# Column sums of attention probabilities: from GpSimd additions to TensorE products in four quadrants of one bank

## The chip, the cores and the metric

The kernel runs on one core of a Trainium2 chip. The metric is the device time of one execution in microseconds (us), from inputs in HBM to the output in HBM. Engines are named as in the profile: PE is TensorE, DVE is VectorE, ACT is ScalarE, POOL is GpSimd, SP is SyncE, which here only issues transfers.

## What is computed

The input `x` has 8 batches of 512 tokens with 128 channels. Four blocks follow each other, each with a residual: a causal attention with 16 heads of 8 channels and a distance bias, a gated feed-forward layer, a second attention over a compressed set of keys, and the feed-forward layer again. The second attention has to choose 51 of the 512 tokens first, and for that it computes the full attention's probabilities, from which only three statistics are kept:

```python
scores = jax.nn.softmax(jnp.einsum('bhqd,bhkd->bhqk', q, k) * scale, axis=-1)
# inside _heavy_hitter_indices(scores, S):
entropy = -jnp.sum(scores * jnp.log(jnp.clip(scores, 1e-08)), axis=-1)
max_attn = scores.max(axis=-1)
influence = scores.sum(axis=-2)
importance = -entropy.mean(axis=1) * 0.4 + max_attn.mean(axis=1) * 0.3 + influence.mean(axis=1) * 0.3
_, idx = jax.lax.top_k(importance, k)          # k = 51
```

`influence` is the column sum: for each key, the sum of its probabilities over all 512 queries and 16 heads. It is the part that the change computes in another way.

## The kernel before

The program is a software pipeline over the batches, written out by hand. One pass of `one_pass(i, a, p, m, s)` works on up to four batches at once: `p` projects batch i+1, `a` is the causal attention of batch i with its feed-forward layer, `m` is the full attention and the selection for batch i-1, and `s` is the small attention of batch i-2 with its feed-forward layer. Eight passes have the part `m`: the first has no `s`, the next five are the loop body and have all four parts, the seventh has no `p`, the eighth has neither `a` nor `p`. Every pass ends in a barrier of all engines.

Every engine has its own instruction stream in program order, and the streams meet only in semaphores. All of them count the same steps `n` from 0 to 74. Steps 0 to 63 each handle one tile of the full attention: 128 queries of one head against 512 keys (`h, t = n // 4, n % 4`). In a loop pass the other parts are put at fixed steps between them: the last eight heads of the causal row maxima in steps 0 to 7 (DVE line 866, after PE lines 1145 and 1148), the small attention's heads in steps 8 to 20 (PE lines 1397 and 1197), the causal attention in steps 20 to 49 (five tiles in three steps: PE line 1165 with its mask 1167, ACT line 776, PE line 1183), and from step 50 the projection, the layer norms and the feed-forward layers. In step 60 POOL computes the last bf16 parts of the next batch's queries and keys (line 560). SP then writes them to DRAM and reads them back into the causal stacks, 12 transfers of 128 KB each, and the pass doesn't end before these have landed.

One tile of the full attention goes this way:

- PE computes the scores one step ahead, in step n-1 (line 1229), into one of four PSUM banks, the ring 0, 1, 2, 6. It first waits until the tile four before has left the bank: `pe.wait_ge(s_bn, n - RN + 1)`, where `s_bn` counts entropies. The operands lie in partitions 64 and up; those of the causal scores lie in the lower 64.
- DVE takes the row maxima (line 947) at the head of its step n.
- ACT computes the exponentials into one of eight slots of `E` (named `setup` in the profile, line 747) with their row sums `Z`, and then the logarithm of the sums (line 750). POOL makes a threshold from it (line 606).
- DVE computes the entropy's sum from the bank, the threshold and `E` (line 902) in step n+2, directly behind the maxima of that step. After the fourth tile of a head it inverts the sums into `rz` (line 906).
- In step n+6 the slot of `E` is multiplied by `rz`, by ACT for tiles 0 to 13 and 46 to 55 (line 693) and by DVE for the others (line 919), and POOL adds the slot to the sum `psum` (line 580, 60 times in a pass). The four tiles of the last head are scaled and added by DVE (lines 958 and 962).
- When step 63 is over, PE multiplies `psum` and the last head's sum by a column of ones (lines 1311 and 1313). DVE makes the importance, the ranks and the selection from it, and PE gathers the chosen tokens (lines 1327 and 1330).

## Time and profile before

| | |
|---|---|
| median of 3 runs | 2352.26 us |
| all runs | 2352.26, 2664.49, 2349.68 us |
| profiled execution, first to last instruction | 2347.5 us |
| PE busy (matmuls) | 1731.0 us, 74% |
| DVE busy | 1492.3 us, 64% |
| ACT busy | 1121.6 us, 48% |
| POOL busy | 892.7 us, 38% |
| granted PE clock, mean | 0.757 of full speed |

The page gives no other time of the profiled execution than its span; the median of the runs is 4.8 us above that span. A busy share is an average over all stages of all passes. No engine is near 100%, so the table alone doesn't say what bounds the kernel. The granted clock stands at one of two levels, 1.2 GHz (0.50) and 2.4 GHz (1.00); a mean between them tells how a stretch is divided.

### The profile page before, as it was taken

The page shows a single profiled execution, that of the slowest core. Times are in us where ns is not written, and L with a number is a line of the kernel's source. Part 1 is how long each engine was busy: PE and PEld are TensorE (multiplying, and loading weights), DVE is VectorE, ACT ScalarE, POOL GpSimd, SP SyncE. Part 2 cuts the span into 40 slices and gives each one's busy share as a digit, 9 for nine tenths or more (in the row PEclk, how much of TensorE's full clock was granted, in tenths as well). Part 3 has the DMA queues.
Part 4 walks back from the last instruction along what each step waited for, and adds up shares of the span by engine and source line. Part 5 has one row for each costly group of instructions (what it writes and reads, how often), then busy time and mean ns, then how long its engine had stood idle before and what let it go on. Part 6 is the DMA issues. An engine that isn't in the chain of part 4 may idle for free. (4 is left out here: it accounts for less than half of the span.)

```text
span 2347.5 us, 25009 instructions
## 1 busy us (share of the span) xinstructions
PE 1731.0 (74%) x6733; PEld 734.6 (31%) x6733; DVE 1492.3 (64%) x3701; ACT 1121.6 (48%) x2726; POOL 892.7 (38%) x1252
## 2 busy tenths in 40 slices
PE   1686479668986799568976799668977799647537
PEld 1222233333333332333334332433334332322122
DVE  0401388847886677757875677757876677647931
ACT  1033167516772277416672376516672377446603
POOL 2001146513553155514562154514562155425700
PEclk9998559756987599756987589756987589656557
DMA  3002300250004200240005100240005100130010
GB/s 61 13 2 37 53 2 1 38 75 4 1 5 87 29 3 1 50 69 4 1 12 84 24 3 1 46 72 4 1 5 90 20 3 1 24 51 1 5 24 5
DMA packets 64106, 59.35 MB, mean 25 GB/s; under 512 B 10400, under 2 KB 61648, under 8 KB 63952
## 3 DMA queue, kind: packets, MB, share of 16 engines
q1 hardware_dynamic: 63952, 57.57, 15.1%
q8 instruction: 63, 1.03, 0.2%
q14 instruction: 91, 0.75, 0.1%
HBM read 39.10 MB, written 18.27 MB: 24 GB/s over the span
## 5 line engine op out<-in xcount | busy, mean ns | idle before, releaser
L580 POOL TENSOR_TENSOR psum<-psum,setup 128x512 f32<-128x512 f32 x480 | 614.1, 1279 | 55.5 <-ACT setup L693 52.1
L947 DVE TENSOR_REDUCE nmB<-bank 128x1 f32<-128x512 f32 x512 | 348.2, 680 | 290.7 <-PE bank L1229 289.8
L747 ACT ACTIVATE setup<-bank,nmB 128x512 f32<-128x512 f32 x512 | 349.8, 683 | 283.4 <-DVE nmB L947 252.7
L606 POOL TENSOR_TENSOR thr<-lnZ,nmB 128x1 f32<-128x1 f32 x512 | 102.1, 199 | 790.3 <-ACT lnZ L750 786.9
L902 DVE SCALAR_TENSOR_TENSOR junk<-bank,thr,setup 128x512 f32<-128x512 f32 x512 | 378.6, 739 | 20.5 <-POOL thr L606 18.8
L1229 PE MATMUL bank<-k_stacks,q_stacks 48*128 48x512 bf16 x512 | 236.8, 470 | 181.1 <-DMA k_stacks<-part_dram 111.0
L1183 PE MATMUL bank<-pT,vA 128*9 128x512 f32 (+3 forms) x1024 | 342.4, 440 | 10.8 <-ACT ov L686 10.6
L866 DVE TENSOR_REDUCE nm<-bank 128x1 f32<-128x512 f32 (+3 forms) x512 | 225.6, 482 | 127.6 <-PE bank L1148 124.7
L1145 PE MATMUL bank<-k_stacks,q_stacks 52*128 52x512 bf16 (+3 forms) x512 | 217.4, 425 | 120.0 <-PEq L1476 59.2
L776 ACT ACTIVATE pT<-bank 128x512 f32<-128x512 f32 (+1 forms) x384 | 198.8, 521 | 190.9 <-PE bank L1167 188.8
L919 DVE TENSOR_SCALAR setup<-setup,rz 128x512 f32<-128x512 f32 x288 | 195.0, 677 | 0.0
L1229 PEld LDWEIGHTS bank<-k_stacks,q_stacks 48*128 48x128 bf16 x512 | 47.7, 96 | 418.5 <-DVE junk L902 167.7
L1165 PE MATMUL bank<-q_stacks,k_stacks 55*128 55x512 bf16 (+3 forms) x512 | 159.8, 312 | 21.4 <-ACT pT L776 11.9
L1148 PE MATMUL bank<-maskqk,identb 128*128 128x128 bf16 x512 | 143.3, 280 | 0.0
L693 ACT ACTIVATE setup<-setup,rz 128x512 f32<-128x512 f32 x192 | 135.6, 706 | 0.0
L1197 PE MATMUL bank<-p,vsm 115*9 115x512 f32 x256 | 124.6, 722 | 4.4 <-ACT ov L686 3.6
L1167 PE MATMUL bank<-maskkq,identb 128*128 128x128 bf16 x512 | 118.6, 232 | 0.0
L750 ACT ACTIVATE lnZ<-Z 128x1 f32<-128x1 f32 x512 | 103.9, 203 | 16.2
L875 DVE RECIPROCAL rzo<-bank 128x16 f32<-128x16 f32 x64 | 16.3, 254 | 146.6 <-PE bank L1216 146.6
L1145 PEld LDWEIGHTS bank<-k_stacks,q_stacks 52*128 52x128 bf16 x512 | 51.9, 101 | 182.4 <-issue 90.9
L763 ACT ACTIVATE p<-bank 115x512 f32<-115x512 f32 x128 | 72.2, 584 | 66.5 <-PE bank L1397 33.8
L747 ACT ACTIVATION_READ_ACCUMULATOR setup<-bank,nmB 128x1 f32 x512 | 101.7, 199 | 0.0
(184 smaller groups left out, 2370.5 us busy)
## 6 DMA issues: line engine op xcount, KB each, us to landing
part_dram<-part SPq DMA_DIRECT2D x16, 768.0 KB, 3.3
q_stacks<-part_dram SPq DMA_DIRECT2D x96, 128.0 KB
k_stacks<-part_dram SPq DMA_DIRECT2D x96, 128.0 KB
qsm<-part_dram SPq DMA_DIRECT2D x48, 128.0 KB
x<-in_L_attn_a_x_dram SPq DMA_DIRECT2D x8, 256.0 KB, 3.9
x_dram<-x SPq DMA_DIRECT2D x8, 256.0 KB, 10.2
x2s<-x_dram SPq DMA_DIRECT2D x8, 256.0 KB, 11.4
out_dram<-x SPq DMA_DIRECT2D x8, 256.0 KB, 2.3
```

What stands on the lines that cost most here:

```text
L580: pool.tensor_tensor(psum[:, :], psum[:, :], E[:, n % NE, :], ALU.add).then_inc(s_bi, 1)
L747: act.activation(E[:, n % NE, :], RING[n % RN][:, :], ACT.Exp, bias=nmB[:, h, t:t + 1], accum_out=Z[:, h, t:t + 1]).then_inc(s_be, 1)
L776: act.activation(pT[h % 2][:, c * T:c * T + WIDTH[c]], bank[3 + u % 2][:, 0:WIDTH[c]], ACT.Exp).then_inc(s_p[0], 1)
L866: last = dve.tensor_reduce(nm[0][:, t, h:h + 1], bank[a1_bank(u)][:, at:at + (t + 1) * P], AX_X, ALU.max, negate=True)
L902: dve.scalar_tensor_tensor(out=junk[:, :], in0=RING[n % RN][:, :], scalar=thr[:, h, t:t + 1], in1=E[:, n % NE, :], op0=ALU.max, op1=ALU.mu ...
L919: dve.tensor_scalar(E[:, n % NE, :], E[:, n % NE, :], rz[:, h, t:t + 1], None, ALU.mult).then_inc(s_scv, 1)
L947: dve.tensor_reduce(nmB[:, h, t:t + 1], RING[n % RN][:, :], AX_X, ALU.max, negate=True).then_inc(s_bm, 1)
L1145: pe.matmul(bank[a1_bank(u)][:, at:at + (t + 1) * P], qst[0][0:A_SC, h, t * P:(t + 1) * P], kst[0][0:A_SC, h, 0:(t + 1) * P], start=True, ...
L1148: last = pe.matmul(bank[a1_bank(u)][:, at + t * P:at + (t + 1) * P], identb[:, :], maskqk[:, :], start=False, stop=True, skip_group_check= ...
L1165: pe.matmul(bank[3 + u % 2][:, at:at + w], kst[0][0:A_MX, h, k * P:(k + 1) * P], qst[0][0:A_MX, h, k * P:T], start=True, stop=True)
L1183: last = pe.matmul(bank[5][q:q + HD + 1, k * P:T], vA[:, k, h, :], pT[h % 2][:, c * T + at:c * T + at + T - k * P], start=(k == 0), stop=T ...
L1229: pe.matmul(RING[n % RN][:, :], qst[1][0:B_SC, h, t * P:(t + 1) * P], kst[1][0:B_SC, h, :], start=True, stop=True).then_inc(s_bs, 1)
```

## The change

Nobody multiplies the slots of `E` by `rz` any more, and nobody adds them up. Instead PE forms the column sums: for each head, four products with `rz` of one tile as the stationary operand (128 rows, one column) and the raw exponentials of that tile as the moving operand (512 columns, f32). Tile t of a head writes partition 32t of bank 6, which stays one accumulation over all 16 heads. So the four products of a head lie in four different column quadrants of the array. Bank 6 leaves the ring of scores, which has three banks now. At the end ACT copies the bank, and PE adds the four rows by a product with `quads`, a column that is one in partitions 0, 32, 64 and 96 and zero elsewhere. Beside that three things move: the entropy of tile n is computed in step n+1 in place of n+2, it stands at the end of DVE's step and no longer behind the maxima, and the inverted sums of a head come in the next step's head. POOL keeps the thresholds and its other work.

```diff
-        RING = (bank[0], bank[1], bank[2], bank[6])
+        RING = (bank[0], bank[1], bank[2])
+        INFL = bank[6]
...
-        INFL_LAG = 6
+        INFL_LAG = 5
...
-        ON_ACT = [n for n in range(LAST) if n < 14 or 46 <= n < 56]
-        ON_DVE = [n for n in range(LAST) if n not in ON_ACT]
...
+        ENT_FIRST = False
...
-                    def influence(n):
...
-                        pool.tensor_tensor(psum[:, :], psum[:, :], E[:, n % NE, :], ALU.add).then_inc(s_bi, 1)
...
-                    def probabilities(n):
...
-                        act.activation(E[:, n % NE, :], E[:, n % NE, :], ACT.Copy, scale=rz[:, h, t:t + 1]
-                                       ).then_inc(s_sc, 1)
...
-                                act.wait_ge(s_bi, n - NE + 2)
+                                act.wait_ge(s_bi, (n - NE) // NT + 1)
...
+                        if m and n == M_TAIL:
+
+                            act.wait_ge(s_bi, H)
+                            act.activation(infl[:, :], INFL[:, :], ACT.Copy).then_inc(s_icp, 1)
...
-                        if m and 2 <= n < NMAIN + 2:
-                            entropy(n - 2)
-                        if m and n - INFL_LAG in ON_DVE:
-                            probabilities(n - INFL_LAG)
+                        if m and 0 < n <= NMAIN and n % NT == 0:
+
+                            dve.wait_ge(s_be, n)
+                            dve.reciprocal(rz[:, n // NT - 1, :], Z[:, n // NT - 1, :]).then_inc(s_brz, 1)
...
-                                dve.tensor_scalar(E[:, LAST % NE, :], E[:, LAST % NE, :], rz[:, H - 1, 0:1], None,
-                                                  ALU.mult).then_inc(s_last, 1)
-                                for t in range(1, NT):
...
+                        if m and not ENT_FIRST and 0 < n <= NMAIN:
+                            entropy(n - 1)
...
+                    def influence(h):
+
+                        if h == 0:
+                            pe.wait_ge(s_vt[1], 2)
+                        pe.wait_ge(s_brz, h + 1)
+                        for t in range(NT):
+                            last = pe.matmul(INFL[32 * t:32 * t + 1, :], rz[:, h, t:t + 1], E[:, (NT * h + t) % NE, :],
+                                             start=(h == 0), stop=(h == H - 1))
+                        last.then_inc(s_bi, 1)
...
+                        if m and n >= INFL_LAG and (n - INFL_LAG) % NT == 0 and (n - INFL_LAG) // NT < H:
+                            influence((n - INFL_LAG) // NT)
...
+                                pe.wait_ge(s_icp, 1)
+                                pe.wait_ge(s_bn, NMAIN)
                                 for t in range(NT):
-                                    pe.matmul(bank[0][:, t:t + 1], psum[:, t * P:(t + 1) * P], onesf[:, 0:1],
-                                              start=True, stop=False)
-                                    last = pe.matmul(bank[0][:, t:t + 1], E[:, LAST % NE, t * P:(t + 1) * P],
-                                                     onesf[:, 0:1], start=False, stop=True)
+                                    last = pe.matmul(bank[0][:, t:t + 1], infl[:, t * P:(t + 1) * P], quads[:, :],
+                                                     start=True, stop=True)
```

The order of the instructions on two engines of a loop pass shows the moves. First DVE in steps 1 and 2, before; `nmB` are a tile's maxima, `nm` are causal maxima, `junk` is an entropy, `nnm` belongs to the token norms.

```order
L947 TENSOR_REDUCE nmB<-bank 128x1
L866 TENSOR_REDUCE nm<-bank 128x1 x4
L947 TENSOR_REDUCE nmB<-bank 128x1
L902 SCALAR_TENSOR_TENSOR junk,acc<-bank,thr,setup 128x512
L866 TENSOR_REDUCE nm<-bank 128x1 x4
L1037 TENSOR_REDUCE nnm<-bank 16x1
```

The same two steps in the change:

```order
L919 TENSOR_REDUCE nmB<-bank 128x1
L848 TENSOR_REDUCE nm<-bank 128x1 x4
L884 SCALAR_TENSOR_TENSOR junk,acc<-bank,thr,setup 128x512
L919 TENSOR_REDUCE nmB<-bank 128x1
L848 TENSOR_REDUCE nm<-bank 128x1 x4
L1001 TENSOR_REDUCE nnm<-bank 16x1
L884 SCALAR_TENSOR_TENSOR junk,acc<-bank,thr,setup 128x512
```

The entropy went from ahead of the causal maxima to behind them, and the first one is a step earlier.

Then PE in step 33, before. The first row of the step waits for an entropy; the rows behind it are causal scores, their masks and the products with the values.

```order
L1229 MATMUL bank<-k_stacks,q_stacks 128x512 [waits entropy_sums]
L1165 MATMUL bank<-q_stacks,k_stacks 128x384 [waits probabilities0]
L1167 MATMUL bank<-maskkq,identb 128x128
L1165 MATMUL bank<-q_stacks,k_stacks 128x128
L1167 MATMUL bank<-maskkq,identb 128x128
L1183 MATMUL bank<-pT,vA 9x384 [waits probabilities0]
```

The same place in the change:

```order
L1193 MATMUL bank<-k_stacks,q_stacks 128x512 [waits entropy_sums]
L1202 MATMUL bank<-setup,rz 1x512 [waits full_sums_inverted]
L1202 MATMUL bank<-setup,rz 1x512 x3
L1131 MATMUL bank<-q_stacks,k_stacks 128x384 [waits probabilities0]
L1133 MATMUL bank<-maskkq,identb 128x128
L1131 MATMUL bank<-q_stacks,k_stacks 128x128
L1133 MATMUL bank<-maskkq,identb 128x128
L1149 MATMUL bank<-pT,vA 9x384 [waits probabilities0]
```

A group of four products has come between the scores of the full attention and the causal scores, which followed each other before. The groups stand in steps 5, 9, 13 and so on up to 65, 16 in a pass.

## Rows read from the trace of the kernel before

**Rows 1.** Stretches of the fourth pass: busy us (instructions), clock, DMA share, GB/s.

```profile
1049.50:1077.60 28.10, 24.29 (x86) 8.72 (x86) 25.16 (x60) 13.22 (x35) 5.59 (x12) 0.50 0.02 4
1077.60:1112.40 34.80, 31.51 (x112) 13.42 (x112) 19.76 (x52) 27.06 (x66) 17.56 (x24) 0.76 0.02 4
1112.40:1196.60 84.20, 79.74 (x331) 26.02 (x332) 66.77 (x156) 60.37 (x154) 45.16 (x63) 1.00 0.00 1
1196.60:1228.20 31.60, 21.22 (x85) 11.71 (x83) 28.72 (x75) 21.90 (x54) 22.48 (x33) 0.82 0.03 9
1228.20:1263.90 35.70, 18.56 (x76) 13.18 (x76) 20.79 (x62) 9.55 (x17) 10.97 (x13) 0.74 0.49 74
1263.90:1312.40 48.50, 31.37 (x154) 16.42 (x154) 26.31 (x62) 6.47 (x14) 8.82 (x11) 0.57 0.51 83
```

**Rows 2.** End of that pass: POOL's timeline (start, us), and what SP's queue waited for.

```profile
1228.23 2.45 POOL L560 TENSOR_TENSOR part<-rest,part 128x512 bf16<-128x512 f32 x2
...
SPq L539 <- DMA x_dram<-x: 12.3, 1, 12.3
```

**Rows 3.** Groups by line, whole execution: busy us, mean ns, idle before.

```profile
L580 POOL TENSOR_TENSOR psum<-psum,setup 128x512 f32<-128x512 f32 x480 | 614.1, 1279 | 55.5 <-ACT setup L693 52.1
L919 DVE TENSOR_SCALAR setup<-setup,rz 128x512 f32<-128x512 f32 x288 | 195.0, 677 | 0.0
L693 ACT ACTIVATE setup<-setup,rz 128x512 f32<-128x512 f32 x192 | 135.6, 706 | 0.0
L962 DVE SCALAR_TENSOR_TENSOR setup<-setup,rz 128x512 f32<-128x512 f32 x24 | 25.1, 1047 | 0.8
```

**Rows 4.** PE's timeline, products of one head, then of two heads, in two places.

```profile
2292.35 1.88 PE L1197 MATMUL bank<-p,vsm 115*9 115x512 f32 x2
2294.76 2.03 PE L1197 MATMUL bank<-p,vsm 115*9 115x512 f32 x4
...
1104.01 1.02 PE L1197 MATMUL bank<-p,vsm 115*9 115x512 f32 x2 [0.16 <-ACT ov L686]
1104.96 0.39 PE L1229 MATMUL bank<-k_stacks,q_stacks 48*128 48x512 bf16 x1
```

**Rows 5.** PE's timeline in step 36.

```profile
1158.46 0.39 PE L1229 MATMUL bank<-k_stacks,q_stacks 48*128 48x512 bf16 x1
1158.46 0.39 PE L1165 MATMUL bank<-q_stacks,k_stacks 55*128 55x512 bf16 x1
```

**Rows 6.** Timeline of PE and DVE in step 7.

```profile
1074.29 0.61 PE L1145 MATMUL bank<-k_stacks,q_stacks 52*128 52x512 bf16 x1
1075.21 0.74 DVE L902 SCALAR_TENSOR_TENSOR junk<-bank,thr,setup 128x512 f32<-128x512 f32 x1
1075.48 0.50 PE L1145 MATMUL bank<-k_stacks,q_stacks 52*128 52x384 bf16 x1
1075.88 1.82 DVE L866 TENSOR_REDUCE nm<-bank 128x1 f32<-128x512 f32 x4
1075.91 0.29 PE L1148 MATMUL bank<-maskqk,identb 128*128 128x128 bf16 x1
```

**Rows 7.** What PE waited for in steps 8 to 20: us, times, longest.

```profile
PE bank L1397 <- ACT p L763: 2.6, 5, 0.6
```

**Rows 8.** DVE's layer norm of line 856 in step 59, and over the execution (min/median/max).

```profile
1220.80 3.27 DVE L856 TENSOR_SCALAR xn<-x,mv,rstd 128x128 f32<-128x128 f32 x4
...
L856 DVE TENSOR_SCALAR xn<-x,mv,rstd x128: 329/340/1317, 25.1 to 2323.8; 128x128 f32<-128x128 f32 x128
```

**Rows 9.** DVE's timeline in the eighth pass, from one tile's maxima to the next.

```profile
2180.77 0.68 DVE L947 TENSOR_REDUCE nmB<-bank 128x1 f32<-128x512 f32 x1
2181.37 0.73 DVE L902 SCALAR_TENSOR_TENSOR junk<-bank,thr,setup 128x512 f32<-128x512 f32 x1
...
2182.03 0.49 DVE L919 TENSOR_SCALAR setup<-setup,rz 128x512 f32<-128x512 f32 x1
2182.44 0.68 DVE L947 TENSOR_REDUCE nmB<-bank 128x1 f32<-128x512 f32 x1
```

More of the change, by code:

```diff
@@ L61, in hybrid_block @@
         onesf = sb("onesf", [P, P])
+        quads = sb("quads", [P, 1])
         maskqk = sb("maskqk", [P, P], BF16)
@@ L156, in hybrid_block @@
         own = sb("own", [P, NT])
-        psum = sb("psum", [P, T])
+        infl = sb("infl", [P, T])
         imp = sb("imp", [P, NT])
@@ L296, in _ @@
                 sp.dma_start(bo[:, :], b_out.rearrange("(a n) -> a n", a=1).broadcast_to([P, P])).then_inc(s_w, DMA)
-                sp.wait_ge(s_cdve, 2)
+                sp.wait_ge(s_cdve, 4)
                 ones_row = alibi[:, AL:AL + 1, :].broadcast_to([1, H, T])
@@ L371, in _ @@
             def _(dve):
+                dve.memset(quads[:, :], 0.0).then_inc(s_cdve, 1)
+                dve.wait_ge(s_cdve, 1)
+                for q in range(NT):
+                    last = dve.memset(quads[32 * q:32 * q + 1, :], 1.0)
+                last.then_inc(s_cdve, 1)
                 dve.wait_ge(s_const, 3)
@@ L635, in _ @@
                             lows(0)
-                        if m and INFL_LAG <= n < INFL_LAG + LAST:
-                            influence(n - INFL_LAG)
                 @block.scalar
@@ L948, in _ @@
                                               ).then_inc(s_bm, 1)
-                        if m and 2 <= n < NMAIN + 2:
-                            entropy(n - 2)
-                        if m and n - INFL_LAG in ON_DVE:
-                            probabilities(n - INFL_LAG)
+                        if m and 0 < n <= NMAIN and n % NT == 0:
+                            dve.wait_ge(s_be, n)
+                            dve.reciprocal(rz[:, n // NT - 1, :], Z[:, n // NT - 1, :]).then_inc(s_brz, 1)
+                        if m and ENT_FIRST and 0 < n <= NMAIN:
+                            entropy(n - 1)
                         if m:
                             if n == M_TAIL:
-                                dve.wait_ge(s_bn, NMAIN)
-                                dve.wait_ge(s_brz, H)
-                                dve.tensor_scalar(E[:, LAST % NE, :], E[:, LAST % NE, :], rz[:, H - 1, 0:1], None,
-                                                  ALU.mult).then_inc(s_last, 1)
-                                for t in range(1, NT):
-                                    dve.wait_ge(s_last, t)
-                                    dve.scalar_tensor_tensor(out=E[:, LAST % NE, :], in0=E[:, LAST % NE + t, :],
-                                                             scalar=rz[:, H - 1, t:t + 1], in1=E[:, LAST % NE, :],
-                                                             op0=ALU.mult, op1=ALU.add).then_inc(s_last, 1)
                                 dve.wait_ge(s_bn, NMAIN)
@@ L1118, in _ @@
                                 last.then_inc(s_vt[0], 1)
+                        if m and not ENT_FIRST and 0 < n <= NMAIN:
+                            entropy(n - 1)
                 @block.tensor
```

28 lines of the change are left out of this document (1 added, 27 removed).

## The prediction

> **What bounds the kernel.** I began with one pass of the loop, cut into stretches at the steps where other work begins or ends [rows 1]. The columns after the length are PE, PE's weight loads, DVE, ACT and POOL. The pass takes 262.9 us, and three different limits hold in it. In steps 0 to 8 (28.1 us) DVE is busy 25.2 us and PE 24.3 us, with the clock at 0.50. In steps 8 to 20 (34.8 us) and above all in steps 20 to 49 (84.2 us) it is PE: 79.7 of 84.2 us at full clock, 95%. In steps 49 to 60 (31.6 us) it is DVE with 28.7 us. POOL, from which most is taken, is busy 45.2 of the 84.2 us where PE is full. The end of the pass hangs on transfers: POOL's low parts start at 1228.23 [rows 2], the stacks are loaded behind them, DMA is busy half of that stretch on average, and SP's last wait, 12.3 us, is for a transfer [rows 2]. So from the low parts to the next pass's first step runs a fixed chain of about 84 us (35.7 + 48.5), and a loop pass gets shorter or longer by what steps 0 to 60 do, hardly by what happens to the selection behind them.
>
> **The change part by part.** The sum is made against the profiled execution. Its span is 2347.5 us and the median of the runs 2352.26 us, so I add the sum to the median.
>
> What goes, by the groups of lines [rows 3]: 614 us of POOL's additions, 195 us of DVE's and 136 us of ACT's scalings, and the last head's additions, 3 x 1.047 us a pass. Most of it lay beside a full PE. It costs nothing there and brings nothing.
>
> What comes: 16 groups of four f32 products of 512 columns a pass. No row has such a group. The nearest rows are products of the small attention with f32 weights of 9 columns. One head alone holds PE for 0.95 us until the next instruction starts (1104.01 to 1104.96), and takes 1.88 us at half clock; two heads in two quadrants take 2.03 us at half clock [rows 4]. Two quadrants thus run side by side for 0.15 us more. I take 0.95 us for a group at full clock and 2.0 us at half. Below lies a group that costs nearly nothing, 0.3 us, if it overlaps with its neighbours as well; above, four products one behind the other, 4 x 0.95 = 3.8 us. The Trainium skill ("TensorE: Matmul & The Clock Gate", Part 3, packing small matmuls) gives three column tiles a speedup of 2.38, so three would take 1.26 of one. By it a group would hold PE for 1.2 us or more in place of 0.95 us, and the sum would be some 25 us higher; no run here shows three or four quadrants at once.
>
> A group also parts two instructions which now start together: the scores of the full attention use the upper partitions, the causal scores the lower, and both start at 1158.46 with 0.39 us each [rows 5]. Behind a group they no longer share that time. I add 0.3 us where it stands between them.
>
> *Steps 20 to 49*: eight groups (steps 21, 25, up to 49) of 1.25 us are 10 us. PE waits only 4.5 us in this stretch (84.2 less 79.7), and a group can fill a wait only where it comes just before one: I take off 1 us. **+9 us**, between +1 (all waits filled, a group at 0.7) and +28.
>
> *Steps 8 to 20*: one group at half clock (step 9, 2.0 us) and two at full (2.5 us). PE waits 2.6 us for ACT's exponentials here [rows 7], and ACT loses 12 scalings of 0.706 us [rows 3] in this stretch, so 1.5 us of the waits go. **+3 us**.
>
> *Steps 0 to 8*: here the ring matters. Scores of tile n+1 need the entropy of tile n-2. That entropy is now the last thing in DVE's step n-1, behind the four causal maxima, and PE's causal scores of step n stand in PE's queue behind those scores. So PE can begin a step only when DVE has ended the one before, while DVE needs that step's causal tiles. Now PE starts a head while DVE is still at the one before: from the head's first product (1074.29) to the mask of its second tile (1075.91 + 0.29) it takes 1.9 us [rows 6]. In that time DVE has after the change only a tile's maxima (0.60 us, from 2180.77 to 2181.37 [rows 9]) and the first causal maximum (about as long for 512 columns) to do, so it waits 0.7 to 0.8 us a step. Six steps are bound so: +4.5 us. The group in step 5 lies in the same chain: +2 us. **+6.5 us**, between 0 and +9.
>
> *Steps 49 to 60*: DVE's load falls. The layer norm's four operations took 3.27 us in step 59 with POOL's additions beside them, against 4 x 0.34 us at the median [rows 8]: -1.9 us there, and about -0.8 us for the one in step 51. DVE's three scalings in steps 49 to 51 at 0.41 us of its time each (2182.03 to 2182.44 [rows 9]) go, and two of ACT's ahead of the projections' copies: -2.5 us. Against it, the group of step 53 is ahead of the down product (+1.3 us), and PE's scores wait there for an entropy at the end of a longer DVE step (+1.4 us). **-2.5 us**, between -8 and +1.
>
> A pass with the causal attention thus grows by 9 + 3 + 6.5 - 2.5 = 16 us: six such passes with the small attention make 96 us, the first one, whose steps 8 to 20 have no heads of it, 13 us. The seventh has no stacks to load at its end, so it gets something from the shorter way to the selection: -4 us. The eighth has no causal attention. DVE sets its step: 1.67 us (2180.77 to 2182.44), of which 0.41 us is the scaling [rows 9]. Then the chain from maxima over ACT and POOL to the entropy becomes the bound at an estimated 1.35 us, so 20 steps bring -6 us, other steps and the norms -4 us, the last head's four operations at the end -6 us, and the groups in its steps 8 to 20 cost +4 us: -12 us. Sum: 96 + 13 - 4 - 12 = **+93 us**, 2445 us.
>
> **The rivals.**
>
> *PE takes the groups for nothing (faster).* If a group holds PE for at most 0.55 us, the 4.5 us of waits in steps 20 to 49 swallow all eight; that is the point from which this decides. Steps 0 to 20 then stay as they are, the seven passes give 6 us each in steps 49 to 60, and the eighth gives 24 us: 2352 - 42 - 24 = 2286 us. For it speaks the 0.15 us of the second quadrant; against it that a single product of 512 columns holds PE for 0.95 us in [rows 4], and no row shows such a product beside a full-width one. Chance 0.12.
>
> *The clock rises earlier.* PE is busy 24.3 of 28.1 us in steps 0 to 8 and is still granted 0.50 [rows 1]. If the group in step 5 lifts it, the causal tiles come in half the time and the lockstep costs nothing: steps 0 to 8 give +1.5 us, and steps 8 to 20, which run up to step 12 at half clock, -1 us. A pass grows by 7 us, in all 49 - 16 = +33 us: 2385 us. The Trainium skill ("TensorE: Matmul & The Clock Gate", Part 1) says that activity releases the gate. By that rule steps 0 to 8 should be at full clock already; the trace does not agree. So I don't count on it for one more group. Chance 0.13.
>
> *The couplings are weaker than I think.* DVE reaches the entropy without waiting in steps 0 to 8, more of PE's waits are filled, and steps 49 to 60 give 5 us: a pass grows by 5 us, 35 - 20 = +15 us: 2367 us. Chance 0.12.
>
> *Four quadrants run one after the other.* A group costs 4.1 us at full clock and 7.5 us at half. Per pass: 28 us in steps 20 to 49, 14 us in steps 8 to 20, 11 us in steps 0 to 8, 3 us at the end, 56 us; seven passes and 40 us in the eighth give 2784 us. Against it speaks the pair in [rows 4]. Chance 0.08. The change then does not do what its placing in quadrants says.
>
> **The numbers.** The forecast, 2445 us with its own range from 2400 to 2500 us, has 0.55. A run of this kernel can tell 2% (47 us) from no change, so "within" is 2305 to 2399 us. Faster is the first rival, 0.12. Within 2% are the second and third, and a little of the forecast's lower edge: 0.28. Slower is the rest: 0.60. The range from 2330 to 2500 us leaves out the first and the fourth, 0.2.
>
> **What would show it.** In the profile after: rows of the four products with starts close together and about 1 us from the group's first to the next PE instruction; PE still over 95% busy in steps 20 to 49, a stretch of 93 us; steps 2 to 7 at 3.7 us each, with DVE's causal maxima waiting for PE's masks and PE waiting for the entropy; the layer norm of step 59 at 1.4 us; steps of 1.35 us in the eighth pass. The forecast is wrong if the stretch of steps 20 to 49 doesn't grow by at least 5 us, or if steps 0 to 8 stay at 28 us.

## The result: 3.3% slower, and the profile after

The change takes 2425.5 us (median of 2413.66, 2425.5 and 2445.05) against 2352.26 us. The ratio is 1.033, with a 95% interval from 1.028 to 1.039. The profiled execution has a span of 2412.0 us, 64.5 us more than before.

The groups of the page after, those that answer to [rows 3] and the waits beside them (columns: line, engine, operation, count | busy us, mean ns | idle before, what ended it):

```profile
L1193 PE MATMUL bank<-k_stacks,q_stacks 48*128 48x512 bf16 x512 | 234.1, 464 | 249.4 <-DVE junk L884 137.5
L884 DVE SCALAR_TENSOR_TENSOR junk<-bank,thr,setup 128x512 f32<-128x512 f32 x512 | 379.5, 741 | 73.1 <-POOL thr L596 65.8
L1202 PE MATMUL bank<-setup,rz 128*1 128x512 f32 x1024 | 172.8, 754 | 1.8 <-DVE rz L924 1.8
```

POOL's 614 us, DVE's 195 and ACT's 136 us are gone, and PE has products of 172.8 us in their place. PE's busy time as a whole grew by less, from 1731.0 to 1844.9 us, at a mean clock of 0.768 against 0.757. Each f32 product has two records, so 1024 of them are 128 groups. PE's scores wait 137.5 us for DVE's entropies.

The stretches of the fourth pass after, to be read beside [rows 1] (length, then busy us of PE, PE's loads, DVE, ACT, POOL; clock, DMA share, GB/s):

```profile
1078.70:1113.70 35.00, 26.63 (x98) 9.32 (x97) 26.42 (x63) 12.13 (x33) 3.76 (x10) 0.50 0.02 4
1113.70:1148.90 35.20, 34.60 (x136) 13.20 (x137) 20.00 (x53) 22.06 (x57) 4.29 (x13) 0.76 0.01 3
1148.90:1238.10 89.20, 86.05 (x383) 26.56 (x381) 48.00 (x130) 59.31 (x151) 6.85 (x32) 1.00 0.00 1
1238.10:1270.00 31.90, 24.78 (x113) 11.93 (x117) 24.38 (x68) 15.90 (x45) 8.32 (x22) 0.85 0.03 9
```

(The last one ends, as in [rows 1], at POOL's low parts.) Steps 0 to 8 grew from 28.1 to 35.0 us, while PE has only 2.3 us and DVE 1.3 us more to do in them; steps 20 to 49 grew by 5.0 us. In steps 0 to 8 these waits stand (us in total, times, longest), PE's first, then DVE's:

```profile
PE bank L1193 <- DVE junk L884: 7.3, 6, 1.9
PE bank L1111 <- DVE nm L848: 1.1, 1, 1.1
```

```profile
DVE nmB L919 <- PE bank L1193: 9.8, 1, 9.8
DVE nm L848 <- PE bank L1114: 8.4, 14, 2.7
```

PE waits for the entropy six times and DVE for the causal tiles fourteen times: neither is the bound, each waits for the other. (The 9.8 us lie ahead of step 0.)

One group at full clock, PE's timeline (start, us):

```profile
1164.58 0.39 PE L1193 MATMUL bank<-k_stacks,q_stacks 48*128 48x512 bf16 x1
1164.90 1.04 PE L1202 MATMUL bank<-setup,rz 128*1 128x512 f32 x8
1165.87 0.39 PE L1131 MATMUL bank<-q_stacks,k_stacks 55*128 55x512 bf16 x1
```

And one at half clock, in step 5:

```profile
1100.13 0.61 PE L1193 MATMUL bank<-k_stacks,q_stacks 48*128 48x512 bf16 x1 [1.89 <-DVE junk L884]
1100.67 1.89 PE L1202 MATMUL bank<-setup,rz 128*1 128x512 f32 x8
1102.49 0.60 PE L1111 MATMUL bank<-k_stacks,q_stacks 52*128 52x512 bf16 x1
```

From the group's start to the next instruction it is 0.97 us at full clock and 1.82 us at half.

The stretches of e10 and e14 below are read from executions in a slower state, with a mean clock of 0.743 and 0.717; no ratio contains such executions, while the medians of e7, e9, e10 and e14 do.

### The profile page after: what moved, and what is told of

Same layout as the page of the kernel before. It is cut to its first block and busy times, and to the rows that moved or that the text cites. A ratio compares the mean times of both kernels' runs of the same rounds, so it can differ in the third digit from the quotient of the medians.

```text
span 2412.0 us, 24982 instructions
## 1 busy us (share of the span) xinstructions
PE 1844.9 (76%) x7693; PEld 715.4 (30%) x7693; DVE 1282.4 (53%) x3386; ACT 1020.9 (42%) x2542; POOL 283.8 (12%) x764
## 5 line engine op out<-in xcount | busy, mean ns | idle before, releaser
L1193 PE MATMUL bank<-k_stacks,q_stacks 48*128 48x512 bf16 x512 | 234.1, 464 | 249.4 <-DVE junk L884 137.5
L596 POOL TENSOR_TENSOR thr<-lnZ,nmB 128x1 f32<-128x1 f32 x512 | 97.1, 190 | 1491.8 <-ACT lnZ L730 1491.8
L1202 PE MATMUL bank<-setup,rz 128*1 128x512 f32 x1024 | 172.8, 754 | 1.8 <-DVE rz L924 1.8
L1131 PE MATMUL bank<-q_stacks,k_stacks 55*128 55x512 bf16 (+3 forms) x512 | 158.8, 310 | 13.2 <-DMA q_stacks<-nm_dram 9.4
L745 ACT ACTIVATE p<-bank 115x512 f32<-115x512 f32 x128 | 73.6, 591 | 106.4 <-PE bank L1163 61.0
L1131 PEld LDWEIGHTS bank<-q_stacks,k_stacks 55*128 55x128 bf16 x512 | 47.5, 93 | 165.9 <-issue 87.3
L891 DVE TENSOR_REDUCE nm<-bank 128x4 f32<-128x460 f32 x128 | 72.0, 629 | 45.7 <-PE bank L1248 45.7
```

The source lines that it names most:

```text
L1131: pe.matmul(bank[3 + u % 2][:, at:at + w], kst[0][0:A_MX, h, k * P:(k + 1) * P], qst[0][0:A_MX, h, k * P:T], start=True, stop=True)
L1193: pe.matmul(RING[n % RN][:, :], qst[1][0:B_SC, h, t * P:(t + 1) * P], kst[1][0:B_SC, h, :], start=True, stop=True).then_inc(s_bs, 1)
L1202: last = pe.matmul(INFL[32 * t:32 * t + 1, :], rz[:, h, t:t + 1], E[:, (NT * h + t) % NE, :], start=(h == 0), stop=(h == H - 1))
```

## The experiments

Kernels are compared by the ratio to the kernel before on the same chip, with its 95% interval, and by the length of the stretches, read from the starts of DVE's maxima in each trace. Passes 2 to 6 are loop passes; a range gives the smallest and largest of them. The last column is steps 0 to 63 of the eighth pass. Medians of different kernels can't be set against each other to the microsecond: the kernel before had 2369.38 us beside e1 to e4, 2356.33 us beside e5 and e8 to e10, 2350.04 us beside e7, e11 and e14, and 2354.04 us beside e16. The stretches vary too. Up to step 63, e7 runs the same instructions as the kernel before, and its eighth pass takes 131.6 us against 134.0 us, because the clock rose earlier (mean clock of steps 8 to 20: 0.76 against 0.65). So a difference of 2 to 3 us in the last column, read from one execution each, shows nothing by itself.

| kernel | ratio | 0-8 | 8-20 | 20-49 | 49-60 | eighth |
|---|---|---|---|---|---|---|
| before | 1 | 28.1 | 34.7-37.4 | 84.2-87.1 | 28.2-29.0 | 134.0 |
| after | 1.033 | 35.0 | 35.2-38.3 | 89.2 | 29.3-29.6 | 137.9 |
| e1, small groups | 1.013 (1.005-1.020) | 35.0 | 32.8-38.2 | 84.2-85.7 | 26.7-29.9 | 128.4 |
| e2, one quadrant | one run | 37.0-38.7 | 39.3-43.7 | 106.4 | 31.2-32.9 | 164.9 |
| e3, entropy first | 1.012 (0.999-1.024) | 29.9 | 30.6-36.8 | 88.6 | 26.2-27.8 | 133.0 |
| e4, before with three banks | 1.064 (1.056-1.071) | 35.5 | 36.4-38.6 | 88.7-91.4 | 33.6-35.6 | 153.4 |
| e5, before without sums | 0.969 (0.961-0.978) | 28.1 | 31.8-36.4 | 83.0-85.9 | 22.5-24.1 | 120.0 |
| e7, last head on PE | 1.006 (1.002-1.010) | 28.1 | 34.8-37.1 | 84.2-85.8 | 28.2-29.0 | 131.6 |
| e8, groups behind | 1.006 (1.001-1.010) | 30.0 | 35.3-36.8 | 88.7-90.2 | 27.0 | 130.8 |
| e9, POOL in heads 4-11 | 1.004 (0.999-1.008) | 29.9 | 36.1-39.3 | 84.5-86.0 | 29.0-30.0 | 131.1 |
| e10, e3 without groups | 0.982 (0.974-0.991) | 28.7 | 32.8-38.4 | 83.5-85.0 | 26.0-27.6 | 128.3 |
| e11, groups in bf16 | 0.995 (0.992-0.999) | 28.7 | 33.3-39.1 | 84.7-87.6 | 25.1-28.1 | 128.9 |
| e14, e7 and ACT | 1.003 (0.999-1.007) | 28.1 | 35.0-37.8 | 84.3-93.6 | 28.5-29.6 | 138.0 |
| e16, POOL in heads 4-9 | 0.993 (0.990-0.996) | 29.9 | 36.0-39.6 | 83.1 | 27.8-29.3 | 137.8 |

**e1: the groups' own price.** In the change:

```diff
+                        if 0 < h < H - 1:
+                            pe.matmul(INFL[0:1, 0:1], rz[:, h, 0:1], E[:, (NT * h) % NE, 0:1], start=False,
+                                      stop=False).then_inc(s_bi, 1)
+                            return
```

> The change with the groups of heads 1 to 14 cut to one product of one column (the column sums of these heads are left out); semaphores, ring and order stay. Theory, the groups' own time on PE is most of the loss: 112 groups go, each of which holds PE for 0.97 us at full and 1.82 us at half clock. In a loop pass steps 20 to 49 go from 89.2 back to 84 to 85 us, steps 0 to 8 from 35.0 to 32 us (step 5 back to 4 us), and the pass gets 10 to 13 us shorter; the eighth pass, steps 0 to 63, goes from 137.9 to 127 us or less. Time 2425 - 95 = 2330 us, between 2310 and 2350. Rival, the ring of three and the late entropy are most of it: the groups fill waits, and the time stays above 2380 us.

Median 2385.86 us, above the 2380 us of the rival. Steps 20 to 49 lost 3.5 to 5 us and the eighth pass 9.5 us, as expected; steps 0 to 8 couldn't change, because the group in step 5 is that of head 0, which was left whole. That part of the expectation was an error in the edit. By the ratios, which are uncertain by 0.7 and 0.5 points, 14 of the 16 groups are worth 2.0 of the 3.3 points, and 1.3 points stay without them although POOL, DVE and ACT have been relieved. So these groups cost about 49 us, half of what was expected, and the ring and the entropy have a share that this run can't give.

**e2: the quadrants.**

```diff
-                            last = pe.matmul(INFL[32 * t:32 * t + 1, :], rz[:, h, t:t + 1], ...
-                                             start=(h == 0), stop=(h == H - 1))
+                            last = pe.matmul(INFL[0:1, :], rz[:, h, t:t + 1], ...
+                                             start=(h == 0 and t == 0), stop=(h == H - 1 and t == NT - 1))
```

`quads` has its only one in partition 0 here.

> The change with all four products of a group on partition 0 of the bank, so in one quadrant. Theory, the four quadrants run side by side: in one quadrant a group holds PE for 4 x 0.95 = 3.8 us at full clock and 7.5 us at half in place of 0.97 and 1.82, and the time grows by 280 to 380 us, to about 2750 us. Rival, placement does nothing and the products overlap in any case: a group stays at 0.97 us and the time at 2425 us.

2661.41 us, one run. PE's timeline of a group:

```profile
1256.54 3.59 PE L1202 MATMUL bank<-setup,rz 128*1 128x512 f32 x8
1260.07 0.28 PE L1131 MATMUL bank<-q_stacks,k_stacks 55*128 55x256 bf16 x1
```

It holds PE for 3.53 us in place of 0.97. The quadrants do run side by side. The time grew by 236 us, less than expected. One reason is the clock: in the fourth pass it rises in the middle of the group of step 5, which takes 5.28 us to the next instruction, not 7.5.

```profile
1193.34 5.35 PE L1202 MATMUL bank<-setup,rz 128*1 128x512 f32 x8
1198.62 0.39 PE L1111 MATMUL bank<-k_stacks,q_stacks 52*128 52x512 bf16 x1
```

The mean clock of the whole execution is 0.819 against 0.768 in the change. How much groups that fall into waits take off besides wasn't separated.

**e3: the place of the entropy.**

```diff
-        ENT_FIRST = False
+        ENT_FIRST = True
```

> The change with the entropy directly behind the maxima in every step of DVE, as before the change, but of the tile before. Theory, the late entropy makes the lockstep of steps 2 to 7: their waits of PE for the entropy (7.3 us in the fourth pass) go, and steps 0 to 8 fall from 35.0 to 31 us, 28.1 of before and the group of step 5. But the entropy of the tile before needs POOL's threshold, which comes 1.5 to 1.7 us behind its maxima, so in short steps DVE waits for it; steps 20 to 49 and the eighth pass don't change by more than 2 us each. Seven passes of -4 us: 2397 us, between 2385 and 2415. Rival, three banks alone make the lockstep, whatever the place of the entropy: steps 0 to 8 stay at 34 us or more and the time at 2425 us.

Median 2381.38 us, a little faster than expected. Steps 0 to 8 fell by 5.1 us as the theory says (4 expected); steps 49 to 60 fell by 2.1 us as well (means of passes 2 to 6) and the eighth pass by 4.9 us, where I expected nothing. PE's waits for the entropy in steps 0 to 8 are gone. One switch that isn't needed for the groups costs about 2.1% (1.033 against 1.012, whose interval is wide: 0.999 to 1.024).

**e4: the ring alone.**

```diff
-        RING = (bank[0], bank[1], bank[2], bank[6])
+        RING = (bank[0], bank[1], bank[2])
```

> The kernel before with a ring of three banks in place of four, and nothing else. Theory, the entropy two tiles back at the head of DVE's step is early enough for three banks: PE's scores wait for DVE's entropy of the same step, which is over 1.4 us into it. Steps 0 to 8 grow by 0 to 2 us, steps 20 to 49 not at all, steps 49 to 60 and the eighth pass (where PE waits 34.5 us for entropies already) by 0 to 3 us: time 2352 + 15 = 2367 us, between 2352 and 2390. Rival, the ring is most of the loss: steps 0 to 8 at 34 us or more, time over 2400 us.

Median 2506.48 us, 6.4% slower: a miss by 140 us, and more than the whole change costs. PE's waits in steps 0 to 8, in steps 49 to 60 and in the eighth pass, in this order:

```profile
PE bank L1229 <- DVE junk L902: 10.8, 6, 2.5
```

```profile
PE bank L1229 <- DVE junk L902: 10.1, 7, 3.4
```

```profile
PE bank L1229 <- DVE junk L902: 62.4, 45, 4.0
```

In the eighth pass the kernel before has 34.5 us of this wait. With three banks and the entropy two tiles back, the scores that DVE reads at the head of step n+1 can start only when DVE is through the first two operations of step n. PE and DVE then alternate wherever DVE has much to do.

**e5: the relief alone.** In the kernel before (also without ACT's wait for the additions):

```diff
-                        if m and n - INFL_LAG in ON_DVE:
-                            probabilities(n - INFL_LAG)
...
-                            if n - INFL_LAG in ON_ACT:
-                                probabilities(n - INFL_LAG)
...
-                        if m and INFL_LAG <= n < INFL_LAG + LAST:
-                            influence(n - INFL_LAG)
```

> The kernel before without the scalings and POOL's additions of 15 heads (their column sums are left out); four banks, the entropy two tiles back and the last head's four operations stay. It shows what the relief of POOL, DVE and ACT is worth alone. Theory, the relief pays only where DVE is the bound: steps 0 to 8 stay at 28.1 us, steps 20 to 49 at 84 us, steps 49 to 60 fall from 28.4 to 25 us, steps 0 to 63 of the eighth pass from 134 to 122 us. 7 x 3.5 + 12 = -36 us, ratio to the kernel before 0.985, between 0.975 and 0.995. Rival, the relief brings nothing anywhere, since the last head's operations and the transfers set the ends: ratio 1.00.

Median 2275.0 us, 3.1% faster: the relief is worth twice what was expected. Steps 20 to 49 stayed as they were (85.3 us against 84.8, means of passes 2 to 6), as expected. The gain is in steps 49 to 60 (23.5 against 28.5 us) and in the eighth pass. DVE's timeline in the eighth pass, which answers to [rows 9]:

```profile
2100.07 0.69 DVE L942 TENSOR_REDUCE nmB<-bank 128x1 f32<-128x512 f32 x1
2100.68 0.74 DVE L897 SCALAR_TENSOR_TENSOR junk<-bank,thr,setup 128x512 f32<-128x512 f32 x1
2101.34 0.08 DVE L897 DVE_READ_ACCUMULATOR junk<-bank,thr,setup 128x1 f32 x1
2101.34 0.69 DVE L942 TENSOR_REDUCE nmB<-bank 128x1 f32<-128x512 f32 x1
```

A step takes 1.27 us in place of 1.67.

**e10: e3 without groups.**

```diff
+                        if h < H - 1:
+                            pe.matmul(INFL[0:1, 0:1], rz[:, h, 0:1], E[:, (NT * h) % NE, 0:1], start=True,
+                                      stop=True).then_inc(s_bi, 1)
+                            return
```

> The kernel with the entropy first (e3) with the groups of heads 0 to 14 cut to one product of one column (the column sums of these heads are left out). Against e3 it is the price of the groups, against e5 that of the ring of three with the entropy one tile back. Theory, a group's time on PE is what it costs: steps 20 to 49 fall from 88.6 to 84 us, steps 0 to 8 from 29.9 to 28 us, the eighth pass from 133 to 125 us; 7 x 8 + 8 = 64 us less than e3, ratio to the kernel before 0.985, between 0.975 and 0.995, the same as e5: the ring of three costs nothing once the entropy is early. Rival, the ring still costs: steps 0 to 8 stay at 29.9 us and the ratio at 1.00 or more.

Median 2312.49 us. Against e3 the groups of 15 heads cost 3.0%; the ratio is as forecast, but not equal to that of e5. So three banks cost 1.3% (0.982 against 0.969) even with the entropy early, above all in steps 49 to 60 and in the eighth pass. The two intervals overlap a little (0.974 to 0.991, 0.961 to 0.978). And e10 differs from e5 in more than the ring and the entropy's place: the last head's sums are PE's and no longer DVE's, and a product of one column stands in place of each group. The 1.3% contain that.

**e8: the lost sharing.** From e3, the group at the end of PE's step:

```diff
-                        if m and n >= INFL_LAG and (n - INFL_LAG) % NT == 0 and (n - INFL_LAG) // NT < H:
-                            influence((n - INFL_LAG) // NT)
...
                                 tokens_by(wqkvT[:, 2 * P:3 * P], 0, 0, bank[5])
+                        if m and n >= INFL_LAG and (n - INFL_LAG) % NT == 0 and (n - INFL_LAG) // NT < H:
+                            influence((n - INFL_LAG) // NT)
```

> The kernel with the entropy first (e3), and the group of four products at the end of PE's step, behind the causal tiles, in place of between the scores and these. Theory, the scores and the causal scores share their time again: 0.3 us less for each of about 8 groups in steps 20 to 49, which fall from 88.6 to 86.5 us, and the time falls by 15 to 20 us against e3: ratio to the kernel before 1.004. Rival, the group only moves in front of the next scores and the rest of PE's order sets what is shared: steps 20 to 49 stay within 0.5 us of 88.6 and the ratio at 1.012.

Median 2361.28 us, but steps 20 to 49 stayed at 88.7 us or more: the rival's sign. The intervals of e8 and e3 overlap, so no gain is shown. The trace says why. PE from its scores of tile 22 to those of tile 46, in e3 and then in e8, six groups in each:

```profile
1129.91:1202.81 72.90, 71.72 (x319) 22.24 (x319) 37.86 (x95) 47.68 (x120) 5.53 (x25) 1.00 0.00 1
1124.53:1196.34 71.81, 70.10 (x319) 22.38 (x319) 37.49 (x95) 47.62 (x120) 5.57 (x25) 1.00 0.00 1
```

Here e8 does gain 1.1 us, with 1.6 us less of PE's busy time. But PE's waits for ACT in steps 20 to 49 grew from 1.8 to 3.3 us, and at the end of the stretch nothing is left of the gain.

**e11: the price is columns.** From e3:

```diff
-                            last = pe.matmul(INFL[32 * t:32 * t + 1, :], rz[:, h, t:t + 1], E[:, (NT * h + t) % NE, :],
+                            last = pe.matmul(INFL[32 * t:32 * t + 1, :], rzb[:, h, t:t + 1],
+                                             E[:, (NT * h + t) % NE, :].bitcast(BF16)[:, 1::2],
```

> The kernel with the entropy first (e3), whose groups read only the upper half of each f32 of E as a bf16 (so the column sums are less precise), with the inverted sums in bf16. 512 columns pass once and not four times. Theory, the price of a group is PE's time for its columns: it holds PE for 0.3 us at full and 0.5 us at half clock in place of 0.97 and 1.82; steps 20 to 49 fall from 88.6 to 84 to 85.5 us, the eighth pass from 133 to 129 us, and the time by 45 us against e3: ratio to the kernel before 0.99, between 0.983 and 0.998. Rival, most of the price is the switch between products of different form and the lost sharing: a group still holds PE for 0.7 us or more, steps 20 to 49 stay above 87 us, ratio above 1.003.

Median 2342.78 us. A group on PE:

```profile
1126.30 0.40 PE L1205 MATMUL bank<-setup,rzb 128*1 128x512 bf16 x4
1126.63 0.39 PE L1134 MATMUL bank<-q_stacks,k_stacks 55*128 55x512 bf16 x1
```

0.33 us, and 0.52 us at half clock: a third of the f32 group. The ratio is within its range. Steps 20 to 49 fell to between 84.7 and 87.6 us, less far than the 84 to 85.5 us expected. The price is PE's time for the columns, not a switch between forms. The less precise sums can change which tokens are chosen, so this isn't a replacement.

**e9 and e16: groups only where PE has room.** From e3, with the scalings and POOL's additions of the kernel before for the heads 4 to 11 or 4 to 9, where PE is full:

```diff
+        ON_POOL = range(4 * NT, 12 * NT)
+        GH = [h for h in range(H) if NT * h not in ON_POOL]
+        ON_ACT = [n for n in ON_POOL if n >= 46]
+        ON_DVE = [n for n in ON_POOL if n < 46]
...
-                        if m and n >= INFL_LAG and (n - INFL_LAG) % NT == 0 and (n - INFL_LAG) // NT < H:
+                        if m and n >= INFL_LAG and (n - INFL_LAG) % NT == 0 and (n - INFL_LAG) // NT in GH:
```

> The kernel with the entropy first (e3), and the heads 4 to 11, whose groups would stand in steps 21 to 49, by scalings on DVE and ACT and additions on POOL as in the kernel before; heads 0 to 3 and 12 to 15 keep the groups on PE. Three banks. Theory, eight groups of 0.97 us and their lost sharing leave the stretch where PE is the bound: steps 20 to 49 fall from 88.6 to 84 to 85 us, the rest stays, 7 x 4 = 28 us less than e3, and a little lost in the eighth pass: ratio to the kernel before 1.000, between 0.99 and 1.01. Rival, POOL's additions of 1.28 us again stand ahead of its thresholds, DVE's entropy of the tile before waits for these, and with three banks PE waits for the entropy: steps 20 to 49 stay above 87 us and the eighth pass grows from 133 to over 140 us: ratio 1.015 or more.

Median 2360.49 us. Steps 20 to 49 came down, but steps 49 to 60 rose by 2.3 us (means) beside the late additions. e16 ends them two heads earlier:

```diff
-        ON_POOL = range(4 * NT, 12 * NT)
+        ON_POOL = range(4 * NT, 10 * NT)
```

> As e9, but the heads by scalings (all on DVE) and POOL's additions are 4 to 9 in place of 4 to 11. Heads 10 and 11 have their groups on PE in steps 45 and 49. In the kernel after, the group of step 45 cost nothing, since PE waited 1.6 us for ACT right behind it, and in e9 the additions of the last heads run beside steps 49 to 60, where they cost 2 to 3 us. Theory: steps 20 to 49 stay at 84 to 86 us, steps 49 to 60 fall from 29 to 30 us to 27 us as in e3, 7 x 2 = 14 us less than e9: ratio to the kernel before 0.998, between 0.992 and 1.004. Rival, the groups in steps 45 and 49 cost what the additions did: ratio 1.003 or more.

Median 2338.83 us, ratio 0.993 (0.990 to 0.996): a little faster than the kernel before, and about 4% faster than the change. Steps 20 to 49 of its fourth pass:

```profile
1119.50:1202.60 83.10, 80.15 (x342) 25.86 (x342) 62.59 (x153) 59.05 (x151) 36.30 (x56) 1.00 0.00 1
```

They are shorter than before. Where the 0.7% as a whole lies isn't shown: this execution took 2348.13 us against the median of 2338.83 us, and its loop passes take 263.4 us on average against 262.4 before. Its eighth pass takes 137.8 us against 131.1 us in e9; the difference lies in steps 8 to 20, 38.0 us at a mean clock of 0.67 against 31.9 us at 0.83.

**e7 and e14: the last head.** In the kernel before, DVE's four operations after step 63 by 16 products with E stationary:

```diff
-                                    last = pe.matmul(bank[0][:, t:t + 1], E[:, LAST % NE, t * P:(t + 1) * P],
-                                                     onesf[:, 0:1], start=False, stop=True)
+                                    for j in range(NT):
+                                        last = pe.matmul(bank[0][:, t:t + 1], E[:, LAST % NE + j, t * P:(t + 1) * P],
+                                                         rz[:, H - 1, j:j + 1], start=False, stop=(j == NT - 1))
```

> The kernel before, but the last head's column sums by 16 small products on PE (E of 128 queries x 128 keys stationary, one column of the inverted sums moving) in place of DVE's four operations after step 63 and four products. Theory, the transfers set the end of a loop pass: the store of x goes out 4 to 6 us earlier, the pass doesn't get shorter. Only the seventh pass and the end of the eighth, which have no stacks to load or no transfer at all, get 3 us each: ratio to the kernel before 0.997, between 0.992 and 1.002. Rival, the store of x sets the end of each pass: 3 us in each of eight, ratio 0.990.

Median 2360.3 us, slightly slower, a miss. PE's timeline, first in e7, then in the kernel before:

```profile
1238.56 1.03 PE L1305 MATMUL bank<-rz,setup 128*128 128x1 f32 x8
...
1242.80 3.45 PE L1251 MATMUL bank<-wdT,gated 128*128 128x128 f32 x16
```

```profile
1241.51 0.35 PE L1311 MATMUL bank<-onesf,psum 128*128 128x1 f32 x2 [2.72 <-DVE setup L962]
...
1243.06 0.36 PE L1313 MATMUL bank<-onesf,setup 128*128 128x1 f32 x2
```

Four products with f32 weights of 128 columns hold PE for 0.89 us (1238.56 to 1239.45). The 16 products fill the time in which PE waited 2.72 us for DVE. Counted from the start of the pass, they end 1.2 us later than the eight products before (195.1 us against 193.9). e14 added a change for the eighth pass:

```diff
-        ON_ACT = [n for n in range(LAST) if n < 14 or 46 <= n < 56]
+            ON_ACT = [n for n in range(LAST) if n < 14 or (46 <= n < 56 if a else n % 2 and n < 56)]
```

> As e7, and in the eighth pass ACT does every second scaling of tiles 0 to 55 in place of 24 of them. It is meant to beat both kernels: in the eighth pass DVE sets the step with 1.67 us, of which 0.41 us is the scaling. Theory, the steps without a scaling on DVE take 1.3 us, about half of 30 steps: steps 0 to 63 of that pass fall from 134 to 127 us, and with the gain of e7 the ratio to the kernel before is 0.994, between 0.988 and 1.000. Rival, the chain from the maxima over ACT to POOL's threshold is the bound once ACT has 1.8 us of work in such a step: 134 us and more in that pass, ratio as e7.

Median 2363.78 us, ratio 1.003: a miss, and no gain over e7. The eighth pass took 138.0 us and not 127 (e7: 131.6), but not by the rival's chain. Its steps alternate between 1.27 and 2.6 us. DVE and POOL in one of the long ones:

```profile
2193.68 1.27 POOL L580 TENSOR_TENSOR psum<-psum,setup 128x512 f32<-128x512 f32 x1 [0.42 <-ACT setup L693]
2193.86 1.37 DVE L919 TENSOR_SCALAR setup<-setup,rz 128x512 f32<-128x512 f32 x1
```

In the kernel before, the scaling of [rows 9] starts at 2182.03 and takes 0.49 us. POOL's addition beside it:

```profile
2180.97 1.26 POOL L580 TENSOR_TENSOR psum<-psum,setup 128x512 f32<-128x512 f32 x1
```

In both the scaling ends 0.28 to 0.29 us after POOL's addition does (2195.23 against 2194.95, 2182.52 against 2182.23). It waits for the addition to end, and in e14 it comes right after the addition's start.

## Why the prediction was right in sign, point by point

**Where the 3.3% is.** From before over e5, e10 and e3 to the change, the ratios multiply to it: the relief 0.969, three banks with an early entropy 1.013 (0.982/0.969), the groups 1.030 (1.012/0.982), the entropy at the end of the step 1.022 (1.033/1.012). The product is 1.033 because each kernel is the next one's base, so that it confirms nothing; each factor is uncertain by about one per cent, and in another order the shares are others: with the late entropy, 14 groups cost 2.0% (e1). In us of 2352: -72, +30, +69, +51.

**The price of a group: right.** 0.97 and 1.82 us against 0.95 and 2.0. The rule of the Trainium skill ("TensorE: Matmul & The Clock Gate", Part 3) would have made it 1.2 us or more; the trace does not agree. Four products in one quadrant hold PE 3.53 us and in four 0.97 us: a factor of 3.6 for four tiles, where the page has 2.38 for three column tiles.

**Steps 20 to 49, +9: mechanism right, size too large.** The stretch grew by 5.0 us; its length is 89.2, not 93. The sign that the prediction had set, at least 5 us, stands on its edge: 4.98 us in the fourth pass, and 4.4 us between the means of passes 2 to 6. Three counts were off. From PE's scores of tile 22 to those of tile 46, before and after:

```profile
1117.55:1184.95 67.40, 65.06 (x272) 21.32 (x271) 55.13 (x123) 47.47 (x120) 34.03 (x49) 1.00 0.00 1
1152.90:1225.80 72.90, 71.72 (x319) 22.25 (x318) 38.37 (x98) 47.84 (x120) 5.53 (x25) 1.00 0.00 1
```

Six groups make PE 6.7 us busier, and 1.2 us of waits are filled. With the groups cut to one column (e1), 1.6 us of the 6.7 stay, and e8 has 1.6 us less than e3 here. So the lost sharing is there, at up to 0.4 us for a pair. But full and causal scores started together in 19 steps of the stretch before and in 15 after: only four of the eight groups (steps 21, 25, 29 and 33) parted such a pair. The group of step 45 was free. PE had waited there for ACT; before, then after:

```profile
1184.95 0.39 PE L1229 MATMUL bank<-k_stacks,q_stacks 48*128 48x512 bf16 x1
1186.91 0.39 PE L1165 MATMUL bank<-q_stacks,k_stacks 55*128 55x512 bf16 x1 [1.58 <-ACT pT L776]
...
1226.12 1.04 PE L1202 MATMUL bank<-setup,rz 128*1 128x512 f32 x8
1227.77 0.39 PE L1131 MATMUL bank<-q_stacks,k_stacks 55*128 55x512 bf16 x1 [0.61 <-ACT pT L758]
```

And the group of step 49 starts behind the stretch, at 1238.6. PE's waits in the stretch fell from 4.4 to 1.8 us, not by 1.

**Steps 8 to 20, +3: not confirmed.** +0.4 us in the fourth pass. The stretch varies by 3 us between passes of one kernel with the moment at which the clock rises, so this term can't be judged to that size.

**Steps 0 to 8, +6.5: right.** +6.9 us, by the lockstep: e3, which only moves the entropy, gives 5.1 us of it back (counted as 4.5), and e10 another 1.2 us for the group in step 5 (counted as 2). The other 0.6 us are step 1, 3.0 us long in place of 2.3: DVE has the first entropy there now, which the sum left out. The steps without a group were 3.8 to 4.4 us long, not 3.7. But the ring is a deeper cause than I said. e4 has the entropy at the head of the step and the same 35.5 us. With three banks the entropy must be both one tile back and at the head.

**Steps 49 to 60, -2.5: wrong.** Up to POOL's low parts, the end of the stretch in [rows 1], nothing was gained: 31.6 us before and 31.9 after in the fourth pass, 31.9 in both as means of passes 2 to 6. Up to the maxima of tile 60 they grew by 1.3 us. The relief was there and larger than counted: 5 us in e5, where the layer norm of [rows 8] takes 1.35 us. In the change it takes 1.83 us; the forecast was 1.4. The term that failed is PE's wait for the entropy, counted as 1.4 us. In the stretch up to the low parts, before and then after:

```profile
PE bank L1229 <- DVE junk L902: 4.1, 4, 2.0
PE bank L1193 <- DVE junk L884: 7.9, 5, 2.9
```

It grew by 3.8 us from before to after. By the means of the experiments three banks cost 3.4 us here (e10 against e5), the groups 0.5 us (e3 against e10) and the late entropy 2.1 us (after against e3). The group of step 49 stands here too and was counted in the stretch ahead.

**The end of the pass: right.** From SP's store of the parts to the next step 0 the mean over passes 1 to 5 is 79.9 us before and 79.3 us after, though single passes differ by up to 7 us. In e7 it is 81.4 us. It is the transfers' time; DVE's four operations behind step 63, which the change and e7 leave out, don't set it.

**The eighth pass, -12: wrong.** Steps 0 to 63 took 3.9 us more. DVE's step without scaling was forecast as 1.35 us, and e5 shows 1.27 us and 120.0 us for the pass, a gain of 14. The change gave it back: 8 us for three banks (e10), 5 us for the groups (e3), 5 us for the late entropy, each from one execution and so uncertain by 2 to 3 us. The forecast had 4 us for the groups and put the ring and the late entropy at nothing in this pass. PE is in order there and only one tile ahead:

```profile
2242.28 1.89 PE L1202 MATMUL bank<-setup,rz 128*1 128x512 f32 x8
2244.09 2.08 PE L1224 MATMUL bank<-xnT,wgT 128*128 128x512 f32 x2
2246.10 1.03 PE L1193 MATMUL bank<-k_stacks,q_stacks 48*128 48x512 bf16 x2
2246.74 0.69 DVE L919 TENSOR_REDUCE nmB<-bank 128x1 f32<-128x512 f32 x1 [2.28 <-PE bank L1193]
```

A group at half clock and the gate's products delay the next scores by 3.8 us, and DVE waits 2.28 us. I had counted the groups only in steps 8 to 20. Behind step 63 the pass is 6.5 us shorter (123.8 to 117.3 us), near the 6 us counted for the last head's operations. But e5, which keeps these operations, has 116.8 us there, so that cause isn't shown.

**The sum.** Between the two profiled executions, by the first maxima of each pass:

| part | forecast, us | measured, us |
|---|---|---|
| ahead of the first pass | 0 | -7.0 |
| first pass | +13 | +13.2 |
| passes 2 to 6 | +80 | +50.9 |
| seventh pass | +12 | +9.8 |
| eighth pass to the end | -12 | -2.5 |
| sum | +93 | +64.5 |

The 7.0 us ahead of the first pass can't be put down to the change: e7, which has the instructions of the kernel before there, starts its first pass 9.3 us earlier than it does. A loop pass grew by 10.2 us (272.5 against 262.4, means of passes 2 to 6), not 16: 6.9 us in steps 0 to 8, 0.5 in steps 8 to 20, 4.4 in steps 20 to 49, 1.0 from there to tile 60, and 2.5 us less behind it. The eighth hardly shrank. The errors of the loop passes and of the eighth have opposite signs, so 2445 lay only 20 us above 2425.5; that it came so near is in part luck. "It costs nothing there and brings nothing" holds for steps 20 to 49 (e5), but the relief in the other stretches was counted too small: taken alone, it is 3.1%. The rival of weaker couplings had the direction of the error in steps 20 to 49; the clock didn't rise earlier (0.50 in steps 0 to 8), though it did with the longer groups of e2; the serial quadrants are refuted by e2.

## What to carry to other kernels

Before a buffer is taken from a ring, ask for each consumer order how far the producer may run ahead: here one bank less, alone, cost 6.4%, more than the 3.0% of the groups for which it was taken. An engine that does a small piece of work for another should do it only in the stretches where it has room; with the entropy early, the groups of all heads leave the kernel 1.2% slower than before (e3), and those of ten heads make it 0.7% faster, when the six heads beside the full PE stay on POOL (e16). And measure the relief and the cost apart: here the relief (3.1%) and the groups (3.0%) nearly cancel, and the ring and the late entropy, which the forecast had priced only in steps 0 to 8 and 49 to 60, make the rest.

## What the hardware showed that I had not expected

Four f32 products with one column of weights in four quadrants take as long as one of the small attention with nine: 0.97 us against 0.95.

A DVE scaling, which reads and writes SBUF, doesn't run beside a POOL addition: it is held until that ends (e14, above). In the trace of the kernel before, 201 of DVE's 296 scalings begin during an addition, and not one of them ends less than 0.28 us after it; they take up to 1.54 us, the others at most 0.62 us. The four operations of the layer norm of [rows 8] behave alike: the 61 that meet an addition have a median of 1.22 us, the 67 others 0.34 us. DVE's maxima, which read PSUM, keep 0.68 us with an addition beside them and without, and the entropies 0.74 us. So what a scaling costs is set by when it meets POOL, and [rows 3] show only a mean of 677 ns. The Trainium skill ("SBUF — State Buffer", section "SBUF: two separate sides") describes the pair of ports that the two engines share as an exclusive lock for the whole instruction, and the trace agrees.

The clock level isn't set by the kernel's instructions alone. In two loop passes of one execution of e3, steps 8 to 20 read:

```profile
1095.30:1125.90 30.60, 30.00 (x139) 11.63 (x141) 20.15 (x52) 21.84 (x57) 4.29 (x13) 0.89 0.02 4
1356.60:1392.60 36.00, 35.40 (x139) 14.09 (x141) 20.32 (x52) 21.97 (x57) 4.28 (x13) 0.75 0.01 3
```

The same instructions took 5.4 us longer, where the clock rose later. Taking work from PE can go along with this: in e1 the fifth pass had 38.2 us there, against 35.3 us in the change. Why it rises late in some passes stays open.
